# Value products of two slots in one run, and a turned maximum with weights of full width and height

## The reference, cut to what matters

```python
x = x + tanh(g_xattn[0]) * L0_xattn(ctx, ctx, layernorm(x), mask)   # the part that is changed
x = x + tanh(g_ffn[0]) * L0_ffn(layernorm(x))
x = x + tanh(g_xattn[1]) * L1_xattn(layernorm(x), ctx)
x = x + tanh(g_ffn[1]) * L1_ffn(layernorm(x))

def L0_xattn(values, keys, queries, mask):
    v, k, q = per-head 8x8 projections of values, keys, queries
    energy = einsum('nqhd,nkhd->nhqk', q, k)
    energy = where(mask == 0, -1e20, energy)
    attn = softmax(energy / sqrt(E), axis=3)
    return einsum('nhqk,nkhd->nqhd', attn, v).reshape(N, Sq, E) @ Wo.T + bo
```

## Time and profile before

| | |
|---|---|
| time, median of 3 runs | 1371.87 us (1369.77 to 1372.11) |
| time of the profiled execution | 1371.72 us |
| its span, first to last instruction | 1370.0 us |
| PE busy | 1223.5 us, 89% of the span |
| DVE busy | 1026.2 us, 75% |
| ACT busy | 769.0 us, 56% |
| POOL busy | 395.0 us, 29% |
| value products L725 | 3072 instructions, 113.5 us |
| the turn L692 | 128 instructions, 81.1 to 500.1 us |

### The profile page before, as it was taken

The page is one execution under the profiler, slowest core; times in us unless marked ns, Lnnn a source line. Parts: engine busy times, 40 slices in busy tenths (PEclk is TensorE's granted clock), DMA queues, the critical chain, the costliest instruction groups (busy, mean ns, idle before and its releaser), DMA issues.

```text
span 1370.0 us, 27816 instructions
## 1 busy us (share of the span) xinstructions
PE 1223.5 (89%) x10408; PEld 760.9 (56%) x10408; DVE 1026.2 (75%) x1662; ACT 769.0 (56%) x1013; POOL 395.0 (29%) x248
## 2 busy tenths in 40 slices
PE   0869899999999996788799999999999999999974
PEld 0335565566566566334356666656666666666642
DVE  6656666666666646877888888888888888888877
ACT  0525455555555555455666666666666666666642
POOL 6357666666566415332000000000000000000000
PEclk9979999999999997999999999999999999999996
DMA  5223244234333420010011110011110011110000
GB/s 151 76 78 79 80 114 113 77 101 110 96 90 104 116 58 18 0 46 0 8 38 46 46 44 22 25 45 45 45 45 20 26 44 45 45 45 23 1 0 14
DMA packets 29717, 74.66 MB, mean 54 GB/s; under 512 B 6384, under 2 KB 14960, under 8 KB 29664
## 3 DMA queue, kind: packets, MB, share of 16 engines
q1 hardware_dynamic: 23408, 70.78, 17.7%
q10 hardware_dynamic: 6256, 3.16, 0.9%
HBM read 42.30 MB, written 0.46 MB: 31 GB/s over the span
## 4 chain that ended last, share of the span: by engine, by line
PE 69%; DVE 13%; issue 8%; ACT 7%; ACTq 3%; POOL 0%; DVEq 0%
PE bank L826 13%; PE bank L808 13%; PE bank L768 8%; PE bank L684 7%; PE bank L708 5%; PE bank L712 5%; PE bank L725 4%; DVE bank_max L1497 3%; ACTq L416 2%; DVE region L1639 2%; PE bank L849 2%; ACT region L1141 2%; PE bank L797 2%; DVE e_row L1458 2%; PE bank L1053 2%
## 5 line engine op out<-in xcount | busy, mean ns | idle before, releaser
L1458 DVE CUSTOM_DVE_ANT_0 e_row<-bank,region 112x1500 f32<-112x1500 f32 x128 | 220.1, 1720 | 129.4 <-PE bank L684 128.4
L1176 ACT CAST region<-bank 125x768 f16<-125x768 f32 x224 | 178.7, 798 | 206.2 <-PE bank L768 206.2
L1141 ACT ACTIVATE region<-bank 125x896 f32<-125x896 f32 x192 | 176.0, 917 | 210.0 <-PE bank L712 209.9
L808 PE MATMUL bank<-region 128*128 128x500 f16 x1008 | 234.6, 378 | 14.7 <-ACT e_row L1167 13.3
L1516 DVE TENSOR_TENSOR region<-bank,region 125x768 f16<-125x768 f32 x224 | 209.7, 954 | 25.4 <-ACT region L1176 25.4
L1497 DVE TENSOR_REDUCE bank_max<-bank 128x1 f32<-128x500 f32 x336 | 208.8, 671 | 10.6 <-PE bank L808 10.6
L514 POOL TENSOR_TENSOR region<-c_in,region 125x1536 f16<-125x1536 f32 x16 | 49.7, 3108 | 560.8 <-ACT region L1191 560.8
L768 PEld LDWEIGHTS bank<-ident,e_row 128*125 128x125 f32 x1344 | 175.5, 188 | 31.2 <-DVE region L1516 5.5
L768 PE MATMUL bank<-ident,e_row 128*125 128x128 f32 x1344 | 179.5, 273 | 3.3 <-DVE region L1516 2.6
L1167 ACT ACTIVATE e_row<-bank,neg_max 128x1500 f32<-128x1500 f32 x112 | 169.7, 1515 | 20.2 <-DVE neg_max L1501 20.0
L808 PEld LDWEIGHTS bank<-region 128*128 (+1 forms) x1008 | 93.3, 98 | 115.6 <-issue 11.4
(11 more groups left out here) (212 smaller groups left out, 1471.0 us busy)
## 6 DMA issues: line engine op xcount, KB each, us to landing
c_in<-in_ctx SPq DMA_DIRECT2D x32, 750.0 KB
region<-region SPq DMA_DIRECT2D x64, 192.0 KB, 2.7
region<-in_mask_Bx1xSxS_if SPq DMA_DIRECT2D x32, 328.1 KB
region<-region SPq DMA_DIRECT2D x64, 96.0 KB, 2.5
region<-region SPq DMA_DIRECT2D x8, 750.0 KB
g_w<-region SPq DMA_DIRECT2D x8, 750.0 KB
g_w<-in_L_ffn_rt_gate ACTq DMA_DIRECT2D x1, 1024.0 KB, 9.9
u_w<-in_L_ffn_rt_up ACTq DMA_DIRECT2D x1, 1024.0 KB, 17.4
```

What stands on the lines that cost most here:

```text
L808: last = pe.matmul(bank[:, k, 0:4 * KP], q1[:, ql, b, 128 * t:128 * (t + 1)], c_t1[par][:, cl, 4 * k:4 * k + 4, 0:KP], start=(ql == 0 and ...
L1141: act.activation(p0[:, 2 * i:2 * i + 2, :], ring0("s", h, i)[0:KP, :, 0:HALF_ROWS], ACT.Exp, scale=SCALE0)\
L1176: act.copy(p_high1[grp][:, UC * u:UC * (u + 1), 128 * at:128 * (at + 1)], pair_chunks(unit_no(1, par, ("turn", t, u)), 128)).then_inc(sem( ...
L1458: dve.tensor_tensor_reduce(out=masked.rearrange("p (a k) -> p a k", a=3), in0=bank[0:R0, 0:3, 0:4 * KP], in1=mask_bias[par][:].rearrange(" ...
```

## The change: what it does

Three edits. In the slots 0, 2 and 4 PE issues the value products of that slot and of the next one together, and none in the slots 1, 3 and 5. The four matmuls of the turn have the column of `negc` broadcast to 128 columns as weights, and write all 128 partitions where they wrote partition 96 alone; DVE goes on reading row 96. The flag `none_valid` gets 112 rows where it had 56, and its matmul too writes 128 partitions.

```diff
-        none_valid = sb("none_valid", [S, 1], F16)
+        none_valid = sb("none_valid", [R0, 1], F16)
...
             for t in range(4):
-                last = pe.matmul(place[96:97, 0, R0 * t:R0 * (t + 1)], negc[:, t:t + 1], ident16[0:R0, 0:R0],
+                last = pe.matmul(place[:, 0, R0 * t:R0 * (t + 1)], negc[:, t:t + 1].broadcast_to((R0, 128)), ident16[0:R0, 0:R0],
                                  start=True, stop=True)
             if h == 0:
-                last = pe.matmul(place[0:KP, 1, 0:S], none_valid[:].broadcast_to((S, KP)), ident16[0:S, 0:S],
+                last = pe.matmul(place[:, 1, 0:S], none_valid[:].broadcast_to((R0, 128)), ident16[0:R0, 0:S],
                                  start=True, stop=True)
...
                     for i in range(NP):
-                        if has_before:
+                        if has_before and i % 2 == 0:
                             pe_pv0(pe, *before, i)
+                            pe_pv0(pe, *before, i + 1)
                         if i in (1, 4) and has_after:
                             pe_rows0(pe, after[0], after[1], 4 * after[2] + (1 if i == 1 else 3))
                         pe_st0(pe, b, par, h, i)
...
-                dve.tensor_scalar(none_valid[:], neg_max[0:S, 0:1], MASKED, None, ALU.is_ge)
+                dve.tensor_scalar(none_valid[:], neg_max[0:R0, 0:1], MASKED, None, ALU.is_ge)
```

## The result

The changed kernel takes 1478.20 us (median of 4 runs, 1477.31 to 1480.54) against 1371.61 beside it: a ratio of 1.0782 with an interval of 1.0764 to 1.0801. It is 106.6 us slower. I had said 1372.5, with 1366 to 1380.

The account below looks back on a forecast made before the run. It took DVE's chain to bound three of four steps in second halves, PE and ACT the other. Second halves -2.55, first halves +0.72 and, with projection, +2.58 gave +0.75 us on 1371.72: 1372.5, range 1366 to 1380.

Parts of the forecast that it names:

- R3 to the turn: Last step of a half, from its fourth rows to the turn: set by DVE's scaling, 3.08 us, PE standing 0.88.
- The clock at nothing: PE's granted clock: stays at 1.00, since PE gets gaps of at most 0.9 us; costed at nothing.
- R0 to R0: A whole half, from its first rows to the next half's: second 12.48 us, first 13.50, first with projection 14.40.
- R0 to R3: Second half, from its first rows to its fourth: three steps of 2.86, 3.42 and 2.86 us.
- the rival in which it doesn't wait: First halves: the spread (L737) needn't wait for ACT's copy, each 0.40 us shorter, 1367 us in all; chance 0.15.
- longer lags: Rival: PE's restart at one more place in each half costs 0.15 us more, 4.4 in all, 1377 us; chance 0.17.
- The turn to R0: From the turn to the next half's first rows: 0.22 us, or 0.26 with the flag, instead of 0.29 and 0.45.
- The rival that broadcast weights cost: At the turn: the five loads aren't hidden, about 0.26 us more in each of 29 halves, 1380 us; chance 0.10.
- PE as the bound: Rival: PE bounds the kernel after all, so joined pairs and turn save together 24 us, 1347 us; chance 0.05.
- R1 to R2: From second to third rows of a half: 3.42 us in second halves, 3.82 in first, 4.72 with the projection.
- R0 to R1: From first to second rows of a half: DVE decides in second halves, 2.86 us; 3.10 in first halves.
- R2 to R3: From third to fourth rows of a half: DVE decides in second halves, 2.86 us; PE's in first halves, 3.28.

Follow-up runs that it names:

- experiment 1: The changed kernel with POOL's mask pass also made to wait until DVE has scaled the four maxima: 1374.75 us, ratio 1.0026 to the kernel before.
- experiment 3: The kernel before with only the turn and its flag of full width, value products unchanged: 1367.93 us, ratio 0.9978.
- experiments 9 to 12: One-column scalings on the kernel before: 1364.99 us; with the turn alone 1360.43; with the joining alone 1373.23; on the changed kernel with rows moved in slots 2 and 4: 1371.52.
- by columns: DVE's scaling in four one-column instructions instead of one of four columns; on the changed kernel 1366.57 us, on the kernel before 1364.99.

## Why the prediction was wrong, point by point

**The step that failed** is R3 to the turn, with its sentence "PE stands 0.88 us here, and that is where the work it saved goes" and the one on what is queued behind the turn. It was put at 3.08 us and took 9.15 (276.07 to 285.22), because the scaling, put at the length that it has in the earlier trace rows, was held by POOL's mask pass for 6.26 us. I asked who waits for the turn, and not who is released by the scores that now end 0.8 us earlier. My own sum had PE done at R3 + 2.20, and DVE's scaling only at R3 + 2.98; the measured end of the last scores is R3 + 2.36, and POOL's pass starts 0.19 later. POOL does not occur in the prediction at all. The Trainium skill's rule on the shared pair stood open to me, and the row of 135.57 in the kernel before showed it at work with 4.95 us; I had read four halves from 262 us on, where it doesn't happen. The rivals had no case of this size, so the range could not hold it.

**The clock at nothing** failed with it, as its premise was gaps of 0.9 us: they became 6.8, with half the clock for 3.4 us behind them.

**The rest of the sum** can be read in experiment 1, where the mask pass waits. From R0 to R0 a second half takes 12.43 (260.44 to 272.87), predicted 12.48; a first half 13.60 (246.84 to 260.44), predicted 13.50; one with the projection 14.58 (272.87 to 287.45), predicted 14.40. R0 to R3 is 9.14 in the changed kernel, as summed; R3 to the turn is 3.04 to 3.11, predicted 3.08. The time, 1374.75, is 2.3 over the forecast: the first halves account for 8 x 0.10 + 6 x 0.18 = 1.9, the second halves take 0.7 off, and the 1.1 left over is less than half the width of the interval. PE and ACT of the first half that begins at 246.84:

```profile
249.26 0.83 PE L755 MATMUL bank<-ident,region 128*128 128x128 f16 x12
...
249.93 0.80 PE L684 MATMUL bank<-region 96*128 96x500 f16 x3
250.27 1.44 ACT L1200 COPY region<-bank 128x1536 f16<-128x1536 f16 x1
...
251.76 0.47 PE L737 MATMUL bank<-region 128*128 128x112 f32 x2 [0.26 <-ACT region L1200]
```

The spread does wait for the copy, and starts at R0 + 4.92 as worked out; the wait is 0.26 us and not 0.40, because PE itself came 0.14 later than in my sum. The value products behind it come 0.41 later (252.17) and not 0.31; these are the 0.10 that the first halves are longer than summed. So the rival in which it doesn't wait is out, and so is that of longer lags.

**The turn to R0** was put at 0.22, and 0.26 with the flag. It is 0.21 to 0.31 without it, 0.24 with it (272.63 to 272.87) and 0.30 behind a half with the projection (287.15 to 287.45), 0.08 over my sum: the rest of what that half is longer. The rival that broadcast weights cost is out: the turn alone makes the kernel faster (experiment 3, and 4.6 us or more in experiments 9 to 12).

**PE as the bound** is out as well. The joining saves PE its changes between scores and value products, and still costs 6 to 8 us: by columns, from turn to turn, it makes a first half 13.90 us long that takes 13.64 without it (240.89 to 254.79, and 240.15 to 253.79), one with the projection 14.79 instead of 14.20, and a second half 12.65 instead of 12.59. The loss lies between R1 and R2 of first halves, 3.92 instead of 3.37 and 4.81 instead of 3.93, where the joined products come behind the spread and the spread now waits for the copy (0.26 us; without the joining it does not wait). R0 to R1 and R2 to R3 give back 0.24 and 0.05 there. My sum had these steps at 3.82 and 4.72, and set the gain of the turn against them.

## What to carry to other kernels

When an edit lets an engine finish something earlier, list everything that this end releases, on engines that the edit doesn't touch too, and compare each new start with what runs beside it at that time. A margin of 0.4 us between two engines that share a resource is a condition of the speed, though no wait shows it in the profile; write it as a wait, or take a shape of instruction that needs nothing shared. The place to look in this case was the instruction whose longest execution is over 20 times its median (6.35 us to 0.29 in the changed kernel, 4.95 to 0.20 in the kernel before).

## What the runs showed that I had not expected

- A `tensor_scalar` of 112x4 from on-chip memory to on-chip memory is held for as long as a POOL instruction that was there first: 6.26 us for 0.16. Four of 112x1 on the same numbers take 0.33 us together beside it.
- Its start does not decide whether it is held: 0.10 us at 1.04 us after POOL's start, queued behind a memset that began before it, and 5.39 us at 1.15, kept back until that memset had ended. This fits the order of issue; what happens between issue and start no run shows.
- POOL's difference of two tensors (L560) does it too. DVE and POOL ahead of a turn of a first half in experiment 1, where the scaling ends at 260.17 and POOL's instruction at 260.15:

```profile
257.05 3.10 POOL L560 TENSOR_TENSOR region<-c_in,region 125x1536 f16<-125x1536 f32 x1
...
259.89 0.28 DVE L1471 TENSOR_SCALAR negc<-neg_max 112x4 f16<-112x4 f32 x1
```

It is plainest in the first half of batch 0 of the kernel before, where the scaling starts earlier beside the same instruction, at 94.88: it takes 1.12 us and ends at 96.00, POOL's of 92.87 at 95.98.
